# A fused dual-attention kernel: setup work of the second batch regrouped around the first heads, and the next projections one head earlier

## What is computed

```python
x = L0_attn_x
xn = _layernorm(x, axis=-1)
x = x + _L0_attn_ref(xn, qkv_w, qkv_b, out_w, out_b) + _L0_ffn_ref(xn, ew, act_w, We, be, Wq, Wk, Wv, Wo, ln_g, ln_b)
```

```python
q = apply_rope(q, cos, sin); k = apply_rope(k, cos, sin)
scores = jnp.einsum('bqhd,bkhd->bhqk', q, k) / math.sqrt(Hd)
scores = jnp.where(causal, jnp.finfo(scores.dtype).min, scores)
out = jnp.einsum('bhqk,bkhd->bqhd', softmax(scores), v)
```

```python
q = ew[c, 0] * (nodes[in_q] @ We[eq] + be[eq])
k = ew[c, 1] * (nodes[in_k] @ We[ek] + be[ek])
v = ew[c, 2] * (nodes[in_v] @ We[ev] + be[ev])
nodes[c] = act_w[c] * _mha(q, k, v, Wq[c], Wk[c], Wv[c], Wo[c]) + q
```

## Time and profile before

| | |
|---|---|
| median of 3 runs | 1426.9 us (1423.76 to 1429.07) |
| the profiled execution | 1423.05 us, span 1421.3 us |
| busy: TensorE, its weight loads | 1380.5 us (97%), 935.3 us (66%) |
| busy: VectorE, ScalarE, GpSimd | 1263.0 (89%), 1139.5 (80%), 449.8 (32%) |
| the chain that ended last | TensorE 88%, DMA 4%, VectorE 3% |
| mean granted TensorE clock | 0.991 |

### The profile page before, as it was taken

One profiled execution on the slowest core, in us unless ns is written; L12 is line 12 of the kernel. 1 busy time (PEld: TensorE's weight loads), 2 busy tenths in 40 slices (PEclk: granted clock), 3 DMA queues, 4 the chain that ended last, 5 costly groups with the idle time before them and its releaser, 6 DMA issues.

```text
span 1421.3 us, 60282 instructions
## 1 busy us (share of the span) xinstructions
PE 1380.5 (97%) x26216; PEld 935.3 (66%) x26216; DVE 1263.0 (89%) x1587; ACT 1139.5 (80%) x2133; POOL 449.8 (32%) x936
## 2 busy tenths in 40 slices
PE   6899999999999999999999999999999999999995
PEld 4467777656667666676676766766667666667652
DVE  8889999999989989899899898988989989989895
ACT  3378887688878878888788887887888878878784
POOL 5141115324422433233423332234233432330210
PEclk9899999999999999999999999999999999999998
DMA  8131112343232422333323323233233332321211
GB/s 253 47 116 60 51 59 98 119 142 119 81 127 70 132 97 77 102 109 107 104 78 114 107 74 121 83 123 107 69 101 107 101 107 80 127 98 56 76 38 40
DMA packets 115668, 137.68 MB, mean 97 GB/s; under 512 B 14972, under 2 KB 90109, under 8 KB 115277
## 3 DMA queue, kind: packets, MB, share of 16 engines
q1 hardware_dynamic: 115405, 133.83, 28.7%
HBM read 64.63 MB, written 61.98 MB: 89 GB/s over the span
## 4 chain that ended last, share of the span: by engine, by line
PE 88%; DMA 4%; DVE 3%; SPq 2%; ACT 1%; POOL 1%; issue 1%; ACTq 0%; POOLq 0%; DVEq 0%
PE s L1069 53%; PE cps L1163 26%; PE misc L1069 7%; DMA qs<-mrows 2%; DVE neg_max L971 1%; SPq L431 1%; PE misc L1064 1%; ACT probs L784 1%; DMA dram_raw_b<-csb 1%; PE s L1064 0%; DVE s L967 0%; POOL parts L601 0%; POOL ks L596 0%; POOL full L614 0%; SPq L500 0%
## 5 line engine op out<-in xcount | busy, mean ns | idle before, releaser
L784 ACT ACTIVATE probs<-s 128x512 f32<-128x512 f32 x1792 | 1059.2, 599 | 227.4 <-PE s L1069 166.8
L971 DVE TENSOR_REDUCE neg_max<-s 128x1 f32<-128x1024 f32 x768 | 936.5, 1222 | 62.0 <-PE s L1069 9.1
L1069 PE MATMUL s<-qs,ks 99*32 99x512 bf16 (+2 forms) x7680 | 808.4, 370 | 7.1 <-DMA qs<-mrows 5.1
L1069 PE MATMUL s<-ks,qs 96*32 96x512 bf16 (+2 forms) x7680 | 606.5, 369 | 6.3 <-DMA ks<-dram_qk_a 2.7
L1163 PE MATMUL cps<-probs,vs 128*32 128x256 f32 (+1 forms) x7552 | 591.4, 368 | 0.6 <-ACT probs L784 0.6
L1069 PEld LDWEIGHTS s<-qs,ks 99*32 99x32 bf16 x7680 | 235.8, 94 | 240.6 <-ACT probs L784 96.7
L1163 PEld LDWEIGHTS cps<-probs,vs 128*32 128x32 f32 x7552 | 316.4, 110 | 76.3 <-issue 17.0
L1069 PEld LDWEIGHTS s<-ks,qs 96*32 96x32 bf16 x7680 | 292.5, 97 | 88.6 <-issue 24.5
L633 POOL TENSOR_TENSOR mparts<-neg_max,zeros 128x8 bf16<-128x8 f32 x128 | 26.0, 203 | 796.0 <-DVE neg_max L971 654.3
L967 DVE CUSTOM_DVE_ANT_0 s<-s,mask_q 128x1024 f32<-128x1024 f32 (+7 forms) x256 | 187.8, 785 | 23.5 <-PE s L1069 14.8
L706 POOL TENSOR_TENSOR parts<-full,zeros 128x512 bf16<-128x512 f32 x48 | 61.4, 1280 | 52.2 <-DVE full L949 52.2
(11 more groups left out here) (134 smaller groups left out, 607.6 us busy)
## 6 DMA issues: line engine op xcount, KB each, us to landing
dram_qk_b<-parts SPq DMA_DIRECT2D x48, 384.0 KB, 3.2
qs<-dram_qk_b SPq DMA_DIRECT2D x96, 192.0 KB
ks<-dram_qk_b SPq DMA_DIRECT2D x96, 192.0 KB
dram_qk_b<-parts SPq DMA_DIRECT2D x48, 256.0 KB, 3.2
dram_raw_b<-csb SPq DMA_DIRECT2D x93, 128.0 KB, 4.3
dram_qk_b<-parts SPq DMA_DIRECT2D x48, 128.0 KB, 3.2
vsrc<-srcT SPq DMA_DIRECT2D x12, 512.0 KB, 3.1
ctx_b<-dram_raw_b SPq DMA_DIRECT2D x44, 128.0 KB
```

Of the source, the lines that this page charges most:

```text
L784: nc.scalar.activation(buf[:, lo:hi], s2[bank][:, 0:hi - lo], ACT.Exp, scale=scale).then_inc(exp_done, 1)
L971: last = ve.tensor_reduce(peak, scores, AX.X, ALU.max, negate=True)
L1069: last = te.matmul(dst[c0:c0 + STRIP, :], lhsT[:, c0:c0 + STRIP], rhs, start=start, stop=stop, tile_position=(0, c0))
```

## The change

Rotations 8 to 11 (n = 4 and 5) are made ahead of the first score, in four banks, with their uses on VectorE and all three splits; rotations 12 to 15 are made in heads 0 and 1. Of the products, 4 and 5 go out of the setup into turn 0 of heads 0 and 1, through `misc`, and the wait of the first score for `comp` covers only the four others. products(2) and products(3) stand among the rotations, and biases(0) behind rotation 11 and its use. Bias groups 1, 2 and 3 go from head 0 to heads 2 and 3, the values of batch 1 from heads 4 and 5 to heads 2 and 4.

GpSimd makes its parts of n = 4 and 5 in head 0 and of 6 and 7 in heads 1 and 2 (before: n = 4 to 7 in heads 2 to 5). VectorE's uses of 8 to 11 stand ahead of its 12 scalings. The stores of n = 4 to 7 stay in heads 3 to 6.

In AZ the k and q projections, their splits and their stores come one head earlier; the v projections stay. `load_unit` for the first B head is issued at the top of the last AZ head, ahead of the context's store, and waits for both `pv_done` and `written`.

```diff
-PREP_A_AT = {(2, 2): ("k", 0), (3, 2): ("k", 1), (4, 2): ("q", 0), (5, 2): ("q", 1),
+PREP_A_AT = {(1, 2): ("k", 0), (2, 2): ("k", 1), (3, 2): ("q", 0), (4, 2): ("q", 1),
...
-START_AT = {(0, 0): ("bias", 1), (0, 1): ("bias", 2), (0, 2): ("bias", 3),
-            (0, 4): ("rot", 8), (1, 2): ("rot", 9), (1, 4): ("rot", 10), (2, 2): ("rot", 11),
-            (2, 4): ("rot", 12), (3, 2): ("rot", 13), (3, 4): ("rot", 14), (4, 2): ("rot", 15),
-            (4, 4): ("va", 2), (5, 2): ("va", 3)}
+EARLY = 6
+START_AT = {(0, 0): ("prod", 4), (0, 2): ("rot", 12), (0, 4): ("rot", 13), (1, 0): ("prod", 5), (1, 2): ("rot", 14),
+            (1, 4): ("rot", 15), (2, 2): ("bias", 1), (2, 4): ("va", 2), (3, 2): ("bias", 2), (3, 4): ("bias", 3),
+            (4, 2): ("va", 3)}
...
-CUT_AT = {**{k: {} for k in ("A0", "AL", "BE", "T")}, "AZ": {3: [0], 4: [1], 5: [2], 6: [3]},
+CUT_AT = {**{k: {} for k in ("A0", "AL", "BE", "T")}, "AZ": {2: [0], 3: [1], 4: [2], 5: [3]},
...
-                if k < UP:
+                if k < UP or kind == "AZ":
                     need(sp, pv_done, added(kind, r, k - RING))
-                else:
+                if k == UP:
...
                     need(sp, written, 4 * 3 * 16 * PREPS.after(kind, r))
...
-                    if k < UP - 1 and kind != "T":
+                    if (k < UP - 1 or kind == "AZ") and kind != "T":
                         load_unit(kind, r, k + 1, b)
...
-                    if k == UP - 1 and kind not in ("BE", "T"):
+                    if k == UP - 1 and kind not in ("AZ", "BE", "T"):
                         load_unit(kind, r, UP, b)
...
-                    if kind == "A0" and 2 <= k < 2 + 2 * NCH:
-
-                        n = 2 * NCH + k - 2
-                        rest(n)
-                        low_part(n)
+                    if kind == "A0" and k == 0:
+
+                        for n in range(2 * NCH, EARLY):
+                            rest(n)
+                        for n in range(2 * NCH, EARLY):
+                            low_part(n)
+                    if kind == "A0" and 1 <= k <= 4 * NCH - EARLY:
+                        rest(EARLY + k - 1)
+                        low_part(EARLY + k - 1)
...
-            for n in range(2, NODES):
-                products(n)
+            for n in range(2, 4):
+                products(n, half[n])
+            for n in range(2 * NCH, EARLY):
+                high_part(n)
+            for n in range(2 * NCH, EARLY):
+                middle_part(n)
...
-                        if kind == "A0" and 2 <= k < 2 + 2 * NCH and i == 1:
-                            high_part(2 * NCH + k - 2)
-                        if kind == "A0" and 2 <= k < 2 + 2 * NCH and i == 3:
-                            middle_part(2 * NCH + k - 2)
+                        if kind == "A0" and 1 <= k <= 4 * NCH - EARLY and i == 1:
+                            high_part(EARLY + k - 1)
+                        if kind == "A0" and 1 <= k <= 4 * NCH - EARLY and i == 3:
+                            middle_part(EARLY + k - 1)
...
+            for n in range(2 * NCH, EARLY):
+                for h in range(2):
+                    turn(2 * n + h, (s2[0], s2[1], cps, misc)[(2 * n + h) % 4])
...
-            def products(n):
-
-                need(pe, va_sb, min(n - 1, 2))
-                need(pe, comp_sb, 3 * (n - 3))
+            def products(n, bank):
+
+                if n < 4:
+                    need(pe, va_sb, min(n - 1, 2))
...
+            for m in range(4 * NCH, 2 * EARLY):
+                pe.wait_ge(xt_sb, m // 4 + 1)
+                pe.wait_ge(rot_done, m - 3)
+                rotate(m, (s2[0], s2[1], cps, misc)[m % 4])
+                if m >= 2 * EARLY - 2:
+                    products(m - 2 * EARLY + 4, half[m - 2 * EARLY + 4])
...
-            pe.wait_ge(rot_done, 4 * NCH)
+            pe.wait_ge(rot_done, 2 * EARLY)
             biases(0)
-            for n in range(2, NODES):
-                products(n)
-            pe.wait_ge(comp_sb, 3 * NODES)
+            pe.wait_ge(comp_sb, 3 * 4)
             pe.wait_ge(pool_const, N_CONST)
...
+                if what == "prod":
+                    return comp_sb, 3 * (w + 1)
...
+                elif what == "prod":
+                    pe.wait_ge(bias_used, 1)
+                    products(w, misc)
```

More of the change, by code:

```diff
@@ L741, in products @@
                     nc.scalar.activation(comp[:, (5 * n + w) * D:(5 * n + w + 1) * D],
-                                         half[n % 4][:, w * D:(w + 1) * D], ACT.Copy,
+                                         bank[:, w * D:(w + 1) * D], ACT.Copy,
                                          scale=ewb[:, 3 * n + w:3 * n + w + 1]).then_inc(comp_sb, 1)
@@ L754, in _ @@
             act.wait_ge(wb_in, 16 * 11)
-            products(0)
-            products(1)
+            products(0, half[0])
+            products(1, half[1])
             for g in range(TB // 4):
                 values_a(g)
-            for n in range(2, NODES):
-                products(n)
+            for n in range(2, 4):
[4 more added lines that the diff above has]
+                middle_part(n)
             def phase(kind, r, c, b):
@@ L804, in extra @@
             def extra(kind, r, c, b, ph, what, w):
-                if what == "va":
+                if what == "prod":
+                    products(w, misc)
+                elif what == "va":
                     act.wait_ge(va_ps, w + 1)
@@ L1094, in values_a, with products @@
                 last.then_inc(va_ps, 1)
-            def products(n):
-                need(pe, va_sb, min(n - 1, 2))
-                need(pe, comp_sb, 3 * (n - 3))
+            def products(n, bank):
+                if n < 4:
+                    need(pe, va_sb, min(n - 1, 2))
                 for w in range(3):
-                    last = mm(half[n % 4][:, w * D:(w + 1) * D], we_t_sb[:, (3 * n + w) * D:(3 * n + w + 1) * D],
+                    last = mm(bank[:, w * D:(w + 1) * D], we_t_sb[:, (3 * n + w) * D:(3 * n + w + 1) * D],
                               w4_sb[:, (w * NODES + n) * D:(w * NODES + n + 1) * D])
```

## The result

The changed kernel takes 1421.41 us (median of 20 runs, 1419.22 to 1424.19), the kernel before 1426.12 on the same chip (20 runs, 1422.29 to 1430.09). The ratio is 0.9966, interval 0.9959 to 0.9974, so 4.7 to 4.9 us less, and within 0.5%. The forecast was -3.8 us and 1423.1. The twenty executions of before scatter over 7.8 us and those of after over 5.0, so a single execution of each would not have told them apart.

A forecast was written before the change was run, and what follows sets the result against it. VectorE was taken to bound heads 0 and 1, TensorE heads 2 to 5, with a 1.70 us TensorE wait at the seam. +1.0 - 3.7 - 1.1 = -3.8 us gave 1423.1 by the median, range 1417.5 to 1428.5.

The forecast's parts named there:

- First score: Start of attention A: the first score matmul stays at 37.87 us, with biases(0) ending 0.4 us before the loads land.
- Term 1: Start through head 1: VectorE's first maximum comes at 41.0 instead of 38.65, costing +1.0 us by the end of head 1.
- cold case: Heads 0 and 1: a share of the lower-clock case moves the end of head 1 from 56.8 to 57.1.
- One sign that I had listed as wrong: Heads 0 to 2: a new TensorE wait on comp (products 4 or 5) or bias_used would show the forecast wrong.
- Term 2: Heads 2 to 5: rotations leaving TensorE save 5.8 us, bias groups coming in cost 2.1, so -3.7 us.
- Term 3: Seam from attention A to B: the maxima row leaves SyncE 0.5 us earlier and TensorE waits less, -1.1 us (0 to -1.7).
- the seam is not mended: Rival at the seam: the row lands no sooner behind the two B loads, term 3 nothing, sum -2.7, 1424.2; chance 0.15.
- The slower rival: Before the first score: biases(0) runs at the lower clock, first score 43.0, term 1 +4.3, sum +1.2, 1428.1; chance 0.12.
- The early start: Rival at the start: scalings finish before GpSimd's subtractions, first maximum stays 38.65, sum -7.3, 1419.6; chance 0.15.

The follow-up runs named there:

- scalings in the gap: Changed kernel with six of VectorE's 12 scalings moved ahead of the use of rotation 11, where VectorE idled 1.03 us; 1420.35 us, ratio 0.9953.
- products(4) behind turn 1: Changed kernel with products(4) queued behind the scores of head 0's turn 1 instead of turn 0's; 1420.99 us, ratio 0.9961.
- heads alone: Changed kernel with AZ's k and q projections, their splits and stores, and the first B load back at their old places; 1423.01 us, ratio 0.9968.
- seam alone: Kernel before with only the earlier k and q projections, splits, stores and first B load added; 1426.7 us, ratio 0.9999.
- three together: Changed kernel with six scalings in VectorE's gap, products(4) behind turn 1 and head 31's maxima row ahead of the context's store; 1420.82 us, ratio 0.9956.

## Why the prediction was right

**First score.** 37.35 for 37.87, 0.52 earlier (I had allowed 0.3), and biases(0) ended at 37.4 for 37.5. But the reason is not the one laid out. I had the loads land at 37.8 and 0.4 us of cover for biases(0). The load of k went out 0.75 earlier, and the first score didn't wait for it: biases(0) had no cover left and sets the first score now. The runs in which the clock fell inside biases(0) show it, with the first score right behind its end: 38.37 with the scalings in the gap, 37.81 with products(4) behind turn 1.

**Term 1, +1.0, measured -0.38.** The path was the right one: four scalings were held, as counted, and the first maximum came at 40.46 for 41.0, because GpSimd was through at 39.06 for 39.6. What was mis-sized is VectorE's work behind it. From 40.46 to 55.79 it was busy 14.29 and waited 1.00, where I had 15.0 and 0.8, and 0.3 more for the cold case. I had taken the busy time of head 9, 6.05, for a head's maxima. Short waits stand between them there, and each record counts with its tail. Back to back the records overlap: by their starts, head 1's maxima take 5.65 (49.27 to 53.01 and 53.67 to 55.58), and a use 0.67 where I had 0.75. That is 0.7 of the 1.3 by which head 1 closed earlier than predicted; 0.54 is the first maximum. One sign that I had listed as wrong did show: products(4) waits 1.77 on TensorE for VectorE's bias instruction (40.07), and VectorE 1.00 behind it. The wait had been laid out, and moving it away brought 0.08.

**Term 2, -3.7, measured -3.46.** The heads took 8.72, 7.83, 8.19 and 6.50 for 8.3, 8.0, 8.1 and 6.5. Head 2 is longer by 0.4: there TensorE stood 0.34 for VectorE, and I had laid out no wait. TensorE's busy time in heads 2 to 5 fell from 34.39 to 30.71, by 3.68, which is the term as I had it; its waits grew from 0.31 to 0.53. The late rotations show that it is not the spreading of the work that pays: there all eight rotations stand in heads 0 to 3 and the rest in heads 4 to 6, and the ratio is 0.9989, not 0.9966 (some of the difference, 1.5 us in the profiled execution, is the clock in head 5). What pays is TensorE's time ahead of the first score, into which four rotations go without moving the first score back, and heads 0 and 1, which VectorE bounds and which take four more and two products.

**Term 3, -1.1, measured -0.15.** This step failed, and the rival "the seam is not mended" is what happened. Its first half was exact: the loads at 256.04 (260.1 less the shift), the row 2.1 behind the first load, TensorE ready at 261.31. The landing was wrong. I took a value between 2.97 and 4.30, because the loads would lie further ahead of the row; it was 4.67. In both kernels the two loads and the store, 512 KB, are ahead of the row (in before the store comes first, at 260.75), so issuing the row 0.5 earlier put it behind as much as before. From the first of the three to the landing it is 6.28 in before and 6.76 in after. All the traces with full loads together, by the order in which SyncE issues:

| order | runs | landing after the row's issue | after the first of the three |
|---|---|---|---|
| store, loads, row | before, heads alone | 4.30, 4.49 | 6.28, 6.46 |
| loads, store, row | after, seam alone, scalings, late rotations, products(4) | 4.32 to 4.74 | 6.41 to 6.82 |
| loads, row, store | row ahead of the store, three together | 4.22, 4.60 | 6.04, 6.42 |

The ranges overlap, so the place of the row among them changes little that can be told from the scatter. With the loads cut to 64 KB the row was there in 5.1 of the first and 2.9 of its own issue, below all of them. What is shown is that the bulk of the loads ahead of the row sets its landing; that the store's bytes count by their place isn't, and why the row lands only when the whole batch has been moved, the store behind it too, stays open. The Trainium skill (DMA: Bandwidth & Descriptors, Queues, rings and completion order) says that each DMA engine takes the descriptors of its ring in their order. The run with the small loads agrees with it, and it would have spoken for this rival. The figure of the same page that I weighed (section Anatomy of one DMA), about 2 us fixed, was far from the 4.67.

**The sum.** -0.38 - 3.46 - 0.15 = -3.99 in the stretches, and the mark of head 32 is 4.22 ahead, with the small rest at the projections between. By medians it is 4.7. That the forecast of -3.8 comes so near is in part luck: term 1 came out 1.4 better than forecast and term 3 0.95 worse, and the two errors cancel for the most part. Only term 2 was right in itself. The rest of the walk hides the difference between two single executions: from head 32 to head 127 the profiled execution of after loses 2.66 on that of before, with the same instructions. Most of it lies in the twelve fifth heads of B's phases (36, 44, ... 124): 170.45 in after, 168.20 in before and 169.4 to 170.8 in the eight experiments. One of them, head 52, before and then after:

```profile
492.83:506.90 14.07, 14.07 (x237) 7.88 (x231) 11.11 (x10) 9.93 (x19) 3.43 (x6) 1.00 0.16 52
```

```profile
488.11:502.66 14.55, 14.55 (x245) 8.26 (x241) 11.11 (x10) 10.19 (x19) 3.39 (x6) 1.00 0.16 54
```

TensorE is full at clock 1.00 in both, yet 14.07 became 14.55. Before's profiled execution drew low ones, as its 1423.05 against a median of 1426.12 says. The profiles alone would have given -1.5, so the terms have to be read from marks close to the change, and the sum from the medians. Why these heads scatter stays open; no experiment was made on it.

**The slower rival** had a real mechanism. The clock fell inside or right after one-column matmuls again and again: in biases(0) or at its end (36.0 in the heads alone, 36.2 with the scalings, 36.8 with products(4) moved, 37.5 in after, 38.9 with the row ahead of the store), at 61.1 in head 2 with the small load and at 82.3 in head 5 with the late rotations, both behind bias group 1. Other falls had another setting: at 264.7 one microsecond behind a wait of 1.89, at 32.1 half a microsecond behind one of 3.02 for ScalarE's copy, and in before at 38.4, half a microsecond behind the wait of 2.68 for the first load. The execution with the fall at 32.1 has the first score at 40.25 and closes head 1 at 58.93, 2.8 behind before, where the rival had 60.4 and +4.3; 1.1 of its delay is the longer wait itself. Which execution it strikes is not set by the order of the code, since the heads of that kernel are those of after. The Trainium skill (TensorE: Matmul & The Clock Gate, Part 1) says that the number of slow matmuls at a kernel's start varies from run to run, which agrees in kind; that an idle engine halves the clock does not cover the falls at which TensorE had been busy all along. That the one-column matmuls cause those is an inference from where they fall: none was taken out or widened. Against it, the same bias group 1 in head 2 left the clock at 1.00 in after and in the runs with heads alone, scalings, row ahead of the store, products(4) and three together, where head 2 takes 8.71 or 8.72, and brought it down only with the small load, where it takes 9.84.

**The early start** would have needed the scalings out of the way. Made so, the first maximum came at 39.59 and 39.16, not 38.65, and of its 2.5 at head 1 there came 0.7, and 1.4 with products(4) moved as well. Its -7.3 was not there to be had.

## What to carry over

A setup step inside a head in which TensorE is full is paid in full, and the same step in a stretch that waits for something else costs only what it pushes on other engines; count those engines' instructions one by one, with the neighbour that holds them. A small transfer in a batch of large ones on one queue is priced by the batch, not by its own issue time: here moving its issue, or its place beside the store, changed nothing that stands clear of the scatter, and cutting the loads ahead of it brought 1.7 us at that place. And where an engine sets the pace, its work is taken from the starts of records that stand back to back, not from the busy time of a stretch in which it waits between them.

## What was not expected of the hardware

VectorE's scalings of 128x128 float32 took 0.27 alone and mostly 1.19 beside GpSimd's 128x512 subtractions of 1.14. The prediction had this from two scalings in before; after and the run with the row ahead of the store show it with four for four subtractions, and with the scalings in the gap two were left when GpSimd began, and both were held. While there are scalings left, each GpSimd instruction in the stretch holds one of them. The Trainium skill (SBUF — State Buffer, Who interferes with whom) tells of an exclusive lock that VectorE or GpSimd holds for its whole instruction, and the rows agree.

The granted clock fell to 0.50 with TensorE busy for the whole microsecond, in heads 2 and 5 and at the seam in different kernels. Counting the falls near the first score too, it came back three to ten microseconds later. Where it falls differs between executions of the same code: up to head 5 after and the run with the row ahead of the store are the same, and they closed it at 87.03 and at 90.18 (1.1 of that by the longer wait).
